# Two-layer recurrent block: DMA turns in place of TensorE turns in the tail of layer 0

## The reference

```python
# layer 0
xn = layernorm(x)
s  = layernorm((silu(q k^T) v / S) * u) @ W2 + b2          # u, v, q, k from silu(xn @ W1 + b1)
f  = ff_light(xn) + scatter(ff_heavy(xn[top 1024 rows]))   # rms norm, gelu, two matmuls each
x  = x + s * silu(f)
# layer 1
xn = layernorm(x)
s  = softmax(q k^T / 8) v            # 16 heads of 64, weights rounded to 8-bit steps
h  = silu(xn @ w1) * (xn @ w2)       # 1024 -> 4096
h  = gelu(h @ h1); h = gelu(h @ h2)  # 4096 -> 4096, twice
x  = x + s * silu(h @ w3)            # 4096 -> 1024
```

## Time and profile before

| | us |
|---|---|
| median of 3 runs | 4214.24 (4206.66 to 4214.62) |
| the profiled execution, its own time | 4205.8 |
| its span on the slowest core (core 4) | 4204.2 |
| spans of the eight cores | 4160.4 to 4204.2 |
| TensorE busy | 3919.9 (93%) |
| ScalarE busy | 2097.0 (50%) |
| VectorE busy | 1634.2 (39%) |
| mean granted TensorE clock, core 4 | 0.978 |

### The profile page before, as it was taken

One profiled execution on the slowest core, in us unless ns is written; L12 is line 12 of the kernel. 1 busy time (PEld: TensorE's weight loads), 2 busy tenths in 40 slices (PEclk: granted clock), 3 DMA queues, 4 the chain that ended last, 5 costly groups with the idle time before them and its releaser, 6 DMA issues.

```text
span 4204.2 us, 55884 instructions; the slowest of 8 cores (4160.4 to 4204.2 us)
## 1 busy us (share of the span) xinstructions
PE 3919.9 (93%) x20362; PEld 1681.0 (40%) x20362; DVE 1634.2 (39%) x1775; ACT 2097.0 (50%) x2027; POOL 413.6 (10%) x684
## 2 busy tenths in 40 slices
PE   6799777799899999999999999999999999999999
PEld 3333232344444433344443344444344434433444
DVE  6485411002563435333244434424453342355421
ACT  4799757620450556443355554525654553467101
POOL 3000110101110000001100000020000002100000
PEclk9999988999899999999999999999999999999999
DMA  5466865845443349998433333343333334333794
GB/s 157 79 106 109 120 96 105 126 74 152 144 159 128 130 127 220 218 218 212 144 126 123 112 132 117 137 152 113 122 131 124 122 122 145 133 115 119 230 302 143
DMA packets 146591, 593.24 MB, mean 141 GB/s; under 512 B 22517, under 2 KB 49429, under 8 KB 102677
## 3 DMA queue, kind: packets, MB, share of 16 engines
q0 software_dynamic: 80960, 448.84, 41.5%
q1 hardware_dynamic: 65370, 140.83, 10.3%
HBM read 637.80 MB, written 120.63 MB: 180 GB/s over the span
## 4 chain that ended last, share of the span: by engine, by line
PE 76%; DMA 8%; ACT 8%; issue 4%; DVE 3%; DVEq 2%; POOL 0%; SPq 0%; ACTq 0%; POOLq 0%
PE psP L1697 37%; PE psP L1663 10%; PE psP L1719 5%; ACT pt L786 4%; PE psP L1465 3%; PE psP L1413 3%; PE psP L929 3%; PE psP L987 3%; PE psP L1291 2%; DMA w2s<-W 2%; PE psP L291 2%; DVEq L153 1%; PE psP L779 1%; PE psP L312 1%; DMA wsl<-h2wt 1%
## 5 line engine op out<-in xcount | busy, mean ns | idle before, releaser
L1697 PE MATMUL psP<-hB,wsl 128*128 128x512 bf16 x4096 | 923.3, 382 | 23.1 <-DMA wsl<-h2wt 14.2
L1697 PE MATMUL psP<-hA,wsl 128*128 128x512 bf16 x4096 | 928.8, 381 | 3.7 <-DVE nrm L1337 3.7
L1489 DVE TENSOR_TENSOR accs<-accs,pt 128x2048 f32<-128x2048 f32 x192 | 440.1, 2292 | 897.7 <-ACT pt L1480 897.6
L1697 PEld LDWEIGHTS psP<-hB,wsl 128*128 128x128 bf16 x4096 | 393.9, 98 | 524.5 <-issue 77.4
L1697 PEld LDWEIGHTS psP<-hA,wsl 128*128 128x128 bf16 x4096 | 389.4, 98 | 509.3 <-issue 67.8
L1480 ACT ACTIVATE pt<-psP,nbias 128x1024 bf16<-128x1024 f32 x512 | 542.6, 1111 | 93.6 <-PE psP L1465 86.7
L786 ACT ACTIVATE pt<-psP 128x2048 bf16<-128x2048 f32 x341 | 476.6, 1449 | 80.2 <-PE psP L779 76.4
L1663 PE MATMUL psP<-xn,wsl 128*128 128x512 bf16 x2048 | 452.0, 379 | 3.5 <-ACT sgt L1139 1.8
L1480 ACT ACT_TABLE_LOAD x200 | 256.6, 1283 | 355.8 <-PE psP L1465 338.0
L1704 ACT ACT_TABLE_LOAD x181 | 232.2, 1283 | 259.9 <-PE psP L1697 257.1
L1663 PEld LDWEIGHTS psP<-xn,wsl 128*128 128x128 bf16 x2048 | 199.1, 98 | 242.1 <-issue 7.6
(11 more groups left out here) (229 smaller groups left out, 3243.1 us busy)
## 6 DMA issues: line engine op xcount, KB each, us to landing
wsl<-h1b POOLq DMA_DIRECT2D x125, 1024.0 KB, 5.1
wsl<-h2b POOLq DMA_DIRECT2D x96, 1024.0 KB, 5.1
h1b<-h1wt POOLq DMA_DIRECT2D x32, 1024.0 KB, 11.1
wsl<-h2wt POOLq DMA_DIRECT2D x32, 1024.0 KB, 13.7
h2b<-wsl SPq DMA_DIRECT2D x32, 1024.0 KB, 13.3
wsl<-w1b POOLq DMA_DIRECT2D x96, 256.0 KB, 3.6
wsl<-w2b POOLq DMA_DIRECT2D x96, 256.0 KB, 4.1
wsl<-w3b POOLq DMA_DIRECT2D x24, 1024.0 KB, 5.3
```

The lines of the kernel that those rows point to most:

```text
L1489: VI(lambda v, a=a, sl=sl: v.tensor_tensor(accs[:], a[:], pt2[sl][:], OP.add))
L1697: emitter(lambda t, it=it, i=i, b=b, src=src: t.matmul(pb(b), wsl[i][:, it, :], src[:, it, :], start=(it == 0), stop=(it == 31)))
```

## The change

- `t_turn_x` no longer uses TensorE, PSUM and VectorE: SP issues one DMA with transposition from `xn1b` to its 128 columns of each channel chunk in `xn1` (SBUF to SBUF), through two new semaphores `qtx`. `x_turned`, for which `t_norm` of the next user of the buffer waits, and `xn1_ready`, for which the matmuls wait, are now that DMA's completion.
- `t_turn_sg` becomes `t_store_sg`: POOL stores `sgb` as it is, in token rows, to `sgsp` (now [T, D]). The buffers `sgt` are gone. `t_join` of the next user of `sgb` waits for the store's completion. In the list `first` the step stands right behind `t_stats` of its own tile with weight 0; the turn of `sgb` with weight 4, one tile later, is gone.
- `combo_load` takes `cs` from `sgsp` with a transposing DMA: 512 rows of 128 channels in, 128 x 512 out.
- The weight loading code (`queue_load`, `keep`, `release`, `wsl`, `worder`) stands ahead of the head's tail tiles, as do the first three slots' loads. SP waits ahead of them for the gather of tile 1 (`hg_ld[1]`), where it waited for that of tile 3. The turns of tiles 0 to 3 stand behind these loads in SP's queue.

```diff
--- before.py
+++ after.py
@@ -63,7 +63,7 @@
     dest_d = internal("dest_d", [1, T], I32)
     tab_d = internal("tab_d", [T, 1], I32)
     hrow = internal("hrow", [NHEAVY + 1, D], F32)
-    sgsp = internal("sgsp", [D, T], BF16).rearrange("(c p) t -> p c t", p=128)
+    sgsp = internal("sgsp", [T, D], BF16)
     ctxsp = internal("ctxsp", [D, T], BF16).rearrange("(c p) t -> p c t", p=128)
     gsp = internal("gsp", [D, T], BF16).rearrange("(c p) t -> p c t", p=128)
     xTv = xT.rearrange("(c p) t -> p c t", p=128)
@@ -120,6 +120,12 @@
         st.n += 16
         Q["y"].append(lambda e, o=out, i=in_, h=st.h: e.dma_start(
             out=o, in_=i, allow_slow_non_contiguous=True).then_inc(h, 16))
+        return (st, st.n)
+
+    def y_turn(st, out, in_):
+
+        st.n += 16
+        Q["y"].append(lambda e, o=out, i=in_, h=st.h: e.dma_start(out=o, in_=i, transpose=True).then_inc(h, 16))
         return (st, st.n)
 
     def g_dma(st, out, in_):
@@ -1009,7 +1015,6 @@
     lg = [big(f"lg{i}", kb, [128, D], F32) for i, kb in enumerate((84, 48))]
     sgb = [big(f"sgb{i}", kb, [128, D], BF16) for i, kb in enumerate((92, 56))]
     xn1b = [big(f"xn1b{i}", kb, [128, D], BF16) for i, kb in enumerate((94, 58))]
-    sgt = [big(f"sgt{i}", kb, [128, NCH, 128], BF16) for i, kb in enumerate((124, 60))]
     xn1 = big("xn1", 0, [128, NCH, T], BF16)
     qhg = [stream(f"qhg{i}") for i in range(4)]
     qsg = [stream(f"qsg{i}") for i in range(2)]
@@ -1114,32 +1119,15 @@
             xt_load(tt + 2)
     x_turned = {}
     sg_turned = {}
+    qtx = [stream(f"qtx{i}") for i in range(2)]
     def t_turn_x(tt):
         i = two(tt)
-        b = take()
-        wk("t", tl[tt]["x"])
-        for c in range(NCH):
-            (TN if c < NCH - 1 else TI)(lambda t, c=c, b=b, i=i: t.transpose(
-                pbh(b)[:, c * 128:(c + 1) * 128], xn1b[i][:, c * 128:(c + 1) * 128], eye_bf[:]))
-        x_turned[i] = tok(ct)
-        wk("v", tok(ct))
-        VI(lambda v, tt=tt, b=b: v.tensor_copy(
-            xn1[:, :, tt * 128:(tt + 1) * 128], pbh(b).rearrange("p (c n) -> p c n", c=NCH)))
-        give(b, tok(cv))
-        xn1_ready[tt] = tok(cv)
-    def t_turn_sg(tt):
+        wk("y", tl[tt]["x"])
+        x_turned[i] = xn1_ready[tt] = y_turn(qtx[i], xn1[:, :, tt * 128:(tt + 1) * 128], xn1b[i][:])
+    def t_store_sg(tt):
         i = two(tt)
-        b = take()
-        wk("t", tl[tt]["sg"])
-        for c in range(NCH):
-            (TN if c < NCH - 1 else TI)(lambda t, c=c, b=b, i=i: t.transpose(
-                pbh(b)[:, c * 128:(c + 1) * 128], sgb[i][:, c * 128:(c + 1) * 128], eye_bf[:]))
-        sg_turned[i] = tok(ct)
-        wk("s", tok(ct), st_sg[i])
-        SI(lambda s, b=b, i=i: s.copy(sgt[i][:], pbh(b).rearrange("p (c n) -> p c n", c=NCH)))
-        give(b, tok(cs))
-        wk("g", tok(cs))
-        st_sg[i] = g_dma(qsg[i], sgsp[:, :, tt * 128:(tt + 1) * 128], sgt[i][:])
+        wk("g", tl[tt]["sg"])
+        sg_turned[i] = st_sg[i] = g_dma(qsg[i], sgsp[tt * 128:(tt + 1) * 128, :], sgb[i][:])
 
     for tt in (0, 1):
         hg_load(tt)
@@ -1147,14 +1135,67 @@
         hg_load(tt)
     for tt in (2, 3):
         xt_load(tt)
+
+
+    QT2 = 512
+    NQ2 = T // QT2
+    NW = 3
+    wsl = [big(f"wsl{i}", 96 + 8 * i, [128, 32, 128], BF16) for i in range(NW)]
+    wstreams = {q: [[stream(f"q{q}w{i}_{j}") for j in range(2)] for i in range(NW)] for q in "gy"}
+
+    kept = ("h2", "w3")
+    qkeep = [stream(f"qkeep{i}") for i in range(NW)]
+
+
+    worder = []
+    for Qi in range(NQ2):
+        worder += [(Qi, "in", j) for j in range(16)]
+        for nm, k in (("h1", 32), ("h2", 32), ("w3", 8)):
+            worder += [(Qi, nm, j) for j in range(k)]
+    wpos = {w: n for n, w in enumerate(worder)}
+    wloads = {}
+    wqueued = [0]
+    def queue_load(free):
+        n = wqueued[0]
+        if n >= len(worder):
+            return
+        wqueued[0] += 1
+        Qi, nm, j = worder[n]
+        i = n % NW
+        q = "y" if n < 16 + NW else "g"
+        wk(q, *free)
+        ws = wstreams[q][i]
+        if nm == "in":
+            ld = []
+            for hh in range(2):
+                ht = 2 * j + hh
+                dma(q, ws[hh], wsl[i][:, hh * 16:hh * 16 + 8, :], bdst["w1"][ht, :, :])
+                ld.append(dma(q, ws[hh], wsl[i][:, hh * 16 + 8:hh * 16 + 16, :], bdst["w2"][ht, :, :]))
+            wloads[n] = ld
+        elif nm in kept and Qi == 0:
+            wloads[n] = [g_dma(ws[0], wsl[i][:], bsrc[nm][j, :, :])]
+        else:
+            for st in (qkeep if nm in kept else [qcast[nm]]):
+                wk(q, tok(st))
+            wloads[n] = [dma(q, ws[0], wsl[i][:], bdst[nm][j, :, :])]
+    def keep(n):
+
+        Qi, nm, j = worder[n]
+        if nm in kept and Qi == 0:
+            wk("y", wloads[n][0])
+            wloads[n].append(y_dma(qkeep[n % NW], bdst[nm][j, :, :],
+                                   wsl[n % NW][:].rearrange("p k n -> p (k n)")))
+    def release(n):
+
+        Qi, nm, j = worder[n]
+        queue_load([tok(ct)] + (wloads[n][1:] if nm in kept and Qi == 0 else []))
+    wk("y", *k_C, *st_h, tok(qcast["w1"]), tok(qcast["w2"]), hg_ld[1])
+    for _ in range(NW):
+        queue_load([])
     wk("t", k_rsa, tok(stream("qw2l")), k_W2c[0])
 
     QUAD = ((0, 1, 2, 3), (4, 5, 6, 7))
     ring[:] = []
-    def turn_with(f, tt, b):
-        ring.append(b)
-        f(tt)
-        ring.remove(b)
     for tt in (0, 1):
         t_light(tt, QUAD[tt])
         t_proj(tt)
@@ -1174,27 +1215,23 @@
     t_bias(1, 2)
     for tt in (0, 1):
         t_norm(tt)
-        turn_with(t_turn_sg, tt, 2 + 4 * tt)
+        t_store_sg(tt)
     for tt in (2, 3):
         t_join(tt)
         t_stats(tt)
     t_root(3, 2)
     for tt in (0, 1):
-        turn_with(t_turn_x, tt, 3 + 4 * tt)
+        t_turn_x(tt)
     t_bias(3, 2)
     for tt in (2, 3):
         t_norm(tt)
-        turn_with(t_turn_sg, tt, 0 + 4 * (tt - 2))
+        t_store_sg(tt)
     for tt in (2, 3):
-        turn_with(t_turn_x, tt, 1 + 4 * (tt - 2))
-
-    QT2 = 512
-    NQ2 = T // QT2
-    NW = 3
+        t_turn_x(tt)
+
     xn = xn1
     hA = big("hA", 32, [128, 32, QT2], BF16)
     hB = big("hB", 64, [128, 32, QT2], BF16)
-    wsl = [big(f"wsl{i}", 96 + 8 * i, [128, 32, 128], BF16) for i in range(NW)]
     t1f = [big(f"t1f{i}", 120 + 2 * i, [128, QT2], F32) for i in range(2)]
     gst = [big(f"gst{i}", 124 + i, [128, QT2], BF16) for i in range(2)]
     apos = [126.0]
@@ -1217,8 +1254,6 @@
     wT = {"q": sba("wTq", [128, NCH, 128], BF16), "k": sba("wTk", [128, NCH, 128], BF16),
           "v": sba("wTv", [128, NCH, 256], BF16)}
     qsq = [sba(f"qsq{i}", [128, 512], BF16) for i in range(2)]
-
-    wstreams = {q: [[stream(f"q{q}w{i}_{j}") for j in range(2)] for i in range(NW)] for q in "gy"}
 
 
     qraw = stream("qraw")
@@ -1559,7 +1594,7 @@
         Qs = slice(Qi * QT2, (Qi + 1) * QT2)
         wk("y", cmb["free"][sl])
         y_dma(cmb["ld"][sl], cmb["x"][sl][:], xTv[:, oc, Qs])
-        y_dma(cmb["ld"][sl], cmb["s"][sl][:], sgsp[:, oc, Qs])
+        y_turn(cmb["ld"][sl], cmb["s"][sl][:], sgsp[Qs, oc * 128:(oc + 1) * 128])
         y_dma(cmb["ld"][sl], cmb["c"][sl][:], ctxsp[:, oc, Qs])
         if Qi < NQ2 - 1:
             y_dma(cmb["ld"][sl], cmb["g"][sl][:], gsp[:, oc, Qs])
@@ -1590,56 +1625,6 @@
 
     st_g = [None, None]
     qg = [stream("qg0"), stream("qg1")]
-
-    kept = ("h2", "w3")
...
-    wk("y", *k_C, *st_h, tok(qcast["w1"]), tok(qcast["w2"]), hg_ld[3])
-    for _ in range(NW):
-        queue_load([])
     def main():
@@ -1751,11 +1736,11 @@
             steps.append((4, lambda tt=tt: t_gate(tt)))
             steps.append((4, lambda tt=tt: t_scale(tt)))
         if tt > 4:
-            steps.append((4, lambda tt=tt: t_turn_sg(tt - 1)))
             steps.append((4, lambda tt=tt: t_turn_x(tt - 1)))
         if tt < NTT:
             steps.append((4, lambda tt=tt: t_join(tt)))
             steps.append((6, lambda tt=tt: t_stats(tt)))
+            steps.append((0, lambda tt=tt: t_store_sg(tt)))
             steps.append((6, lambda tt=tt: t_root(tt, 1)))
             steps.append((4, lambda tt=tt: t_bias(tt, 1)))
             steps.append((4, lambda tt=tt: t_norm(tt)))
```

More of the change, by code:

```diff
@@ L1592, in build_program @@
     qg = [stream("qg0"), stream("qg1")]
-    kept = ("h2", "w3")
-    qkeep = [stream(f"qkeep{i}") for i in range(NW)]
-    worder = []
-    for Qi in range(NQ2):
-        worder += [(Qi, "in", j) for j in range(16)]
-        for nm, k in (("h1", 32), ("h2", 32), ("w3", 8)):
-            worder += [(Qi, nm, j) for j in range(k)]
-    wpos = {w: n for n, w in enumerate(worder)}
-    wloads = {}
-    wqueued = [0]
-    def queue_load(free):
-        n = wqueued[0]
-        if n >= len(worder):
-            return
-        wqueued[0] += 1
-        Qi, nm, j = worder[n]
-        i = n % NW
-        q = "y" if n < 16 + NW else "g"
-        wk(q, *free)
-        ws = wstreams[q][i]
-        if nm == "in":
-            ld = []
```

(23 more changed lines are left out.)

## The result

| | before | after |
|---|---|---|
| median, us | 4214.62 (5 runs) | 4259.32 (5 runs) |
| the profiled execution, its own time | 4205.8 | 4252.25 |
| spans of the eight cores | 4160.4 to 4204.2 | 4204.3 to 4250.7 |
| median of the eight spans | 4184.1 | 4230.7 |

The changed kernel is slower: ratio 1.0113, 95% interval 1.0086 to 1.0141. 4204 was forecast, with a range up to 4218.

The account below looks back on a forecast made before the run. TensorE, busy 93% of the span, was taken to bound the kernel. -10.8 +2.5 -3.8 +2 = -10.1 us took the profiled 4205.8 to 4195.7; with the median 8.4 higher, 4204 was given, range 4191 to 4218.

Parts of the forecast that it names:

- Step 1: Layer 1's first matmuls mixed with tail tiles 4 to 15: transposes and `sgt` waits removed from TensorE, -10.8 us.
- Step 2: Price of one 256 KB DMA turn in the tail: 5 us taken, between 2.4 and 8, at 78 ns a piece.
- Step 3: Head, before layer 1's first matmul: it starts later, waiting for tile 3's turn, +2.1, plus 0.4 for slow matmuls: +2.5 us.
- Step 4: Last projection to first quantised weight: last `hA` made earlier, so `raw` loads earlier, -3.8 us; tile 15's turn hidden.
- Step 5: Combination beside the h2 weights: 32 turned `cs` loads in 256-byte runs slow weight landings to 14.1 us, +2 us.
- rival (b): Combination starves the h2 weights: at landings of 20 us, 44 us cost, +32 us in all, 4246; chance 0.15.
- what would show it: The prediction's closing list of trace observations that would show it right or wrong.
- signs of right: Turns about 5 us, stage 162 us, quantised-weight wait 5.9 to about 8, weight turned near 1262, `wsl<-h2b` landing in 10 to 14.
- signs of wrong: SP delaying `wsl` loads TensorE needs; turns over 9 us; `t_norm` waiting for a DMA; over 7 us of `wsl<-h2b` waits.

Follow-up runs that it names:

- experiment 3: Changed kernel, but each `cs` load reads the same 256-byte runs without turning them (values in wrong places); 4184.23 and 4193.67 us.
- experiment 5: Changed kernel, but only every second `cs` load is turned, the others read the same 256-byte runs unturned; 4213.18 us.
- experiment 6: Changed kernel, but products stored in blocks, so that a turned load reads 512 rows of 256 bytes that follow each other directly; 4266.83 us.
- experiment 7: Changed kernel, all `cs` loads turned, but `cx`, `cc`, `cg` loaded for the first ten items only; last score matmul to last h2 matmul 253.3 us (282.5 in changed kernel).
- experiment 8: Changed kernel, but turned `cs` loads read from SBUF (`xn1`) instead of HBM; last score matmul to last h2 matmul 266.0 us (282.5 in changed kernel).
- experiment 9: Changed kernel, but each turned `cs` load reads 128 rows x 512 channels, not 512 x 128; last score matmul to last h2 matmul 276.5 us.
- experiment 4: Kernel before, with only the 32 `cs` loads changed, to turned loads from `xrsp` (other values), tail as before; 4257.63 and 4257.88 us.
- experiment 1: Changed kernel, but `sgb` also turned SBUF to SBUF in the tail, stored channel by channel, and loaded plainly by the combination; 4208.56 us, one time.

## Why the prediction was wrong, step by step

**Step 1, right.** 172.2 to 161.5 us is -10.7, forecast -10.8. The rows of before gave it to a tenth: 20 x 0.45 and the waits for `sgt`. From 1075.7 to 1237.0 on core 3, against the earlier trace rows, TensorE has no gap at all:

```profile
1075.70:1237.00 161.30, 161.28 (x741) 72.88 (x742) 98.10 (x159) 74.93 (x84) 21.35 (x31) 0.99 0.65 188
```

**Step 2, right in size, by luck.** 5.0 was taken. On the three cores where the trace resolves the landings of all 16 turns (5, 6 and 7) they take 5.0 us in the median, 3.1 at least and 13.3 at most; the 7.8 on core 3's page is the median of only two, 4.73 and 10.91. As assumed, a turn moves 1024 packets of 256 bytes (10,240 for the ten turns of the stage), but their price was wrong: 18 ns in the median, not 78. The estimate by the Trainium skill, "DMA: Bandwidth & Descriptors", section "Latency and other measured facts", was 3.0 us, and the fastest turns come to it: 3.06 us for that of tile 15 on core 7.

**Step 3, right in sign, 0.9 us short.** +3.4 on the median core, and +2.5 to +3.9 in the six later kernels with the same turns in the tail (experiments 3 and 5 to 9). The head of core 3 in time, against the earlier trace rows:

```profile
1056.89 14.97 SPq L128 DMA_TRANSPOSE xn<-xn1b  x4
...
1066.72 1.24 ACT L1116 ACTIVATE xn1b<-xt,c_nm,c_rr 128x1024 bf16<-128x1024 f32 x1 [0.66 <-DVE c_nm L1109]
1069.33 1.24 ACT L1116 ACTIVATE xn1b<-xt,c_nm,c_rr 128x1024 bf16<-128x1024 f32 x1 [1.37 <-DMA xn<-xn1b]
...
1075.72 1.87 PE L1648 MATMUL psP<-xn,wsl 128*128 128x512 bf16 x4 [30.40 <-DMA xn<-xn1b]
```

and the chain through it:

```profile
1058.34 10.91 DMA xn<-xn1b
...
1070.64 4.73 DMA xn<-xn1b
```

The turn of tile 1, issued right behind that of tile 0 and beside two row loads `xt` and two stores, took 10.91 us (10.5 to 13.3 on the eight cores; which of its neighbours holds it wasn't tried), and tile 3's `t_norm` waited 1.37 us for it. This wait was named (ScalarE now waits for the turn to land) and costed at nothing for the steady part; in the head, with only 11 us between two users of a buffer, it counts. TensorE didn't run slow for longer, though 0.4 us was added for it: four matmuls take 1.87 us after the start, as before, and the lower clock ends 3.0 us after the start, where it ended 3.9 after it.

**Step 4, right in mechanism, too small.** -6.5 on the median core, where -3.8 was forecast. 4.9 of it is that `raw` is issued earlier, the rest that it lands faster (4.9 us instead of 6.5, both medians of the cores). It is issued 16.5 us after the last projection's end on core 3 (1237.07 to 1253.55), where it was 20.9 on core 4 of the kernel before (1243.86 to 1264.76), and the wait for the turn of tile 15 (issued 1249.93) is hidden, as said:

```profile
1249.93 1.23 SPq L128 DMA_TRANSPOSE xn<-xn1b  x1
...
1253.55 0.34 SPq L112 DMA_DIRECT2D raw<-Wqo  x1
...
1262.32 1.01 PE L1309 MATMUL psP<-eye_bf,wq 128*128 128x128 bf16 x8 [4.75 <-DVE wq L1299]
```

The wait for the weight went down, 5.91 to 4.75, instead of up to 8. The stretch behind it is 3.9 us longer in the table, and TensorE's waits for `wsl<-h2wt` of group 0, loaded from the given weights, are 20.0 us on the median core and were 15.9. But the six kernels with the same turns in the tail have 607.1 to 611.2 us there, beside 608.6 before and 609.1 in experiment 4, whose tail is the old one. So it isn't shown that this stretch loses anything.

**Step 5, the step that failed.** +2 was taken, +49.8 came, and rival (b), given 0.15, is what happened. Its +44 is near by luck: it stood for landings of 20 us, where they were 15.8 in the median and 27.1 at most, and by its own formula 15.8 gives (15.8 + 6.9) / 3 = 7.6 us a tile, that is 14 us over its 21 tiles and 22 over the 33 of the stretch. Four things in the step were wrong.

- The cause of the cost: not pieces, but turning (experiments 3, 4, 6, 9). The short runs, which were held to speak for (b), cost nothing.
- Its size: the DMA time of the stretch is 297.1 us with turned loads and 202.6 with the same runs unturned, 94.5/32 = 2.95 us a load; 1.9 was the difference taken (2.5 less 0.6). And most of it isn't in the turned loads' own packets. Those of 256 bytes go from 18.5 to 35.9 us, those of 1 KB (`cc` and `cg`, which stand right behind `cs` in SP's queue) from 28.4 to 83.2, the weights' of 8 KB from 103.3 to 115.5; `cx`, which stands ahead of `cs`, has packets of 2 KB as the stores have, and these don't grow (49.7 and 41.1).
- The way from DMA time to TensorE, and this weighs most: I let the median landing grow by a third, to 14.1, and compared it with three slots' worth of cover. It grew by half, to 15.8, and even that makes only the 22 us above. The loss isn't the median's alone. Beside the turned loads of experiment 7 the median stays at 10.5 us, the latest landing goes from 14.0 to 23.0, and TensorE waits. That with three slots a load held for 20 us can't be made good by the two behind it, which wait in the same engines, is argued.
- The clock, which the step put at nothing: 12 of the 49.8 us are matmuls at the lower level around the longer waits.

The earlier trace rows had shown the margin: landings up to 16.8 us and 4.8 us of waits already (on core 4; the other seven cores waited 0 to 1.8 us), on a stretch whose DMA share was 0.96. The "against" of rival (b), that a small packet holds a weight packet up less than a long one, had nothing to do with turned loads, whose packets are small too.

Of "what would show it", three signs of right came true (turns near 5 us, the stage in 161.5, the weight turned at 1262.3). The wait for the first quantised weight didn't grow, and `wsl<-h2b` didn't land in 10 to 14 us. Three signs of wrong came: turns landing over 9 us (tile 1's on every core), `t_norm` waiting for a DMA in the head, and more than 7 us of waits for `wsl<-h2b`.

What stays open: why a turned load holds the engines. Source (8), pitch (6) and shape (9) each leave most of the loss. Two rivals were not tried: that the loss hangs on where the turned load stands in SP's queue, or on its sharing that queue with the other loads, and that the eight cores' turns hinder each other.

## What to carry to other kernels

An operation moved from a busy engine to the DMA engines was cheap here where these had room and dear where they were the margin of the stage: with both results turned in the tail (experiment 1) the stage gained 10.1 us, of which the head gave 6.8 back, and 32 turned loads beside the weight stream lost 49.8. Do it once, in the stage with room, and store the turned result, so that the full stage reads it plainly; even so, no version here is shown to be faster than the kernel before. Price a new kind of DMA by a run of it beside the traffic that it will meet, and judge a stream with few buffers by its latest landings, not by the median alone. A DMA share near or over 1 says that packets are in flight, not that they move: read the bytes beside it.

## What the runs showed of the hardware

- Short runs were free: loads in 256-byte runs instead of 1 KB rows left the last h2 stretch at 231.5 us (232.7 with long rows), though the DMA time grew from 192.3 to 202.6.
- A turned load of 128 KB added 2.95 us of DMA time to the same load unturned, more than half of it in the packets of the loads behind it, and cost 1.4 to 1.6 us of TensorE's time beside a full stream of weights. In the 40 us shown it made gaps of 24 to 89 GB/s, where without turning no microsecond was under 202, and held single weight packets for up to 7.9 us. The Trainium skill, "DMA: Bandwidth & Descriptors", section "Rules for kernel authors", says that a transpose next to ordinary DMAs "needs nothing"; that is said of correct data, and of time these runs show the contrary.
- A turn of 256 KB from SBUF to SBUF landed in 3.06 us at best and 5.0 in the median of 48.
- Waits cost more than their length: with 36.9 us of waits for `wsl<-h2b` came 12 us of matmuls at the lower clock.
- SP is held by issuing a turn: 1.22 us at the least in the tail, where a plain weight load mostly takes 0.32 to 0.44. In the last h2 stretch it is 1.6 to 3.0 us in the median by core and up to 11.8, for the plain `cs` loads of before 0.6 to 0.9 and up to 4.7. On core 3:

```profile
3942.25 10.98 SPq L128 DMA_TRANSPOSE cs<-sgsp  x1
3953.28 0.55 SPq L112 DMA_DIRECT2D cc<-ctxsp  x1
```
